# Sigmoid of the second expert choice formed as silu(x) / x in a fused mixture-of-experts kernel on Trainium2

## The reference, cut to what matters

```python
router_in = jnp.concatenate([x_flat, t_flat], axis=-1)
s = jax.nn.sigmoid((router_in @ W_router.T).astype(jnp.float32))
sel_scores = s + router_bias
_, topk_idx = jax.lax.top_k(sel_scores, TOP_K)
s_sel = jnp.take_along_axis(s, topk_idx, axis=1)
denom = jnp.sum(s_sel, axis=1, keepdims=True)
gates = jnp.where(denom > 1e-09, s_sel / (denom + 1e-09), 1.0 / TOP_K)
...
h = jax.nn.gelu(x_flat @ r_w1[e].T, approximate=False)
routed_out = routed_out + h @ r_w2[e].T * gates_full[:, e:e + 1]
```

## Time and profile before

| | us |
| --- | --- |
| median of 3 runs | 898.43 |
| lowest and highest | 897.16 and 898.77 |
| the profiled execution, its own time | 900.26 |
| its span from the first to the last instruction | 898.5 |
| TensorE busy in the span | 876.1 (98%) |
| VectorE busy | 683.7 (76%) |
| ScalarE busy | 576.5 (64%) |
| GpSimd busy | 408.5 (45%) |

### The profile page before, as it was taken

How to read it: one execution, slowest core, us unless ns; L and a number is a source line. 1 busy time by engine, 2 the same in 40 slices (tenths; PEclk the granted TensorE clock), 3 DMA queues, 4 the chain that set the end, 5 groups by cost and what they waited for, 6 DMA issues and landing times.

```text
span 898.5 us, 12685 instructions
## 1 busy us (share of the span) xinstructions
PE 876.1 (98%) x3878; PEld 694.5 (77%) x3878; DVE 683.7 (76%) x1097; ACT 576.5 (64%) x1032; POOL 408.5 (45%) x378
## 2 busy tenths in 40 slices
PE   8999999999999999999999999999999998999996
PEld 5678888878888888888888888888888785777773
DVE  7767777878689786686686686686766976998887
ACT  6878888765555455555555555555555677989896
POOL 7437785025256352253253253253222226755465
PEclk9999999999999999999999999999999999999999
DMA  9588982023023112012012012011010069182650
GB/s 311 174 259 274 321 278 97 1 85 132 19 77 109 36 47 82 1 47 82 1 48 82 1 48 82 5 42 48 7 42 1 0 105 178 36 182 54 158 107 35
DMA packets 35828, 82.96 MB, mean 92 GB/s; under 512 B 4400, under 2 KB 14256, under 8 KB 33840
## 3 DMA queue, kind: packets, MB, share of 16 engines
q1 hardware_dynamic: 35760, 82.15, 31.3%
HBM read 71.13 MB, written 6.83 MB: 87 GB/s over the span
## 4 chain that ended last, share of the span: by engine, by line
PE 77%; DVE 8%; ACT 4%; issue 4%; DMA 4%; SPq 2%; POOL 1%; DVEq 0%; ACTq 0%
PE ps L863 17%; PE ps L882 16%; PE ps L868 16%; PE ps L917 8%; PE ps L919 8%; PE ps L912 8%; DVE HL L1465 2%; DMA CWB<-scratch 2%; ACT HH L1005 1%; PE ps L899 1%; DVE HH L1462 1%; PE ps L897 1%; DVE Hf L1452 1%; POOL HL L1545 1%; SPq L722 1%
## 5 line engine op out<-in xcount | busy, mean ns | idle before, releaser
L999 ACT ACTIVATE Sg<-ps 128x512 f32<-128x512 f32 x288 | 171.7, 597 | 246.3 <-PE ps L882 245.9
L1445 DVE TENSOR_TENSOR Hf<-ps,Sg 128x512 f32<-128x512 f32 x288 | 198.1, 688 | 148.6 <-ACT Sg L999 94.0
L1545 POOL TENSOR_TENSOR HL<-Hf,HH 128x512 fp32r<-128x512 f32 x136 | 182.5, 1349 | 172.3 <-ACT HH L1005 154.6
L1005 ACT ACTIVATE HH<-Hf 128x512 fp32r<-128x512 f32 x346 | 216.4, 625 | 25.0 <-DVE Hf L1445 12.9
L1465 DVE TENSOR_TENSOR HL<-Hf,HH 128x512 fp32r<-128x512 f32 x242 | 215.3, 890 | 4.2 <-ACT HH L1005 3.2
L863 PE MATMUL ps<-XHL,WBH 128*128 128x512 f32 x512 | 203.7, 398 | 1.2 <-DVE Hf L1445 1.2
L882 PE MATMUL ps<-XHL,WBH 128*128 128x512 f32 x512 | 202.2, 395 | 0.0
L868 PE MATMUL ps<-XHL,WBL 128*128 128x512 f32 x512 | 202.0, 395 | 0.0
L1560 POOL TENSOR_TENSOR XT<-XT,TMP 128x512 f32<-128x512 f32 x64 | 84.2, 1316 | 251.4 <-DVE TMP L1341 251.4
L863 PEld LDWEIGHTS ps<-XHL,WBH 128*128 128x128 f32 x512 | 96.1, 188 | 25.2 <-DVE Hf L1445 2.3
L882 PEld LDWEIGHTS ps<-XHL,WBH 128*128 128x128 f32 x512 | 96.0, 188 | 23.1
(11 more groups left out here) (254 smaller groups left out, 1349.0 us busy)
## 6 DMA issues: line engine op xcount, KB each, us to landing
CWB<-scratch SPq DMA_DIRECT2D x68, 256.0 KB, 8.2
CWB<-scratch SPq DMA_DIRECT2D x15, 1024.0 KB, 4.7
GWD<-expert_down SPq DMA_DIRECT2D x21, 576.5 KB, 4.6
GWU<-expert_up SPq DMA_DIRECT2D x21, 514.0 KB, 4.9
ST<-in_wb_dram SPq DMA_DIRECT2D x8, 768.0 KB, 6.3
GX<-XT SPq DMA_DIRECT2D x68, 64.0 KB, 2.8
XT<-in_x_dram SPq DMA_DIRECT2D x8, 256.0 KB, 5.3
expert_up<-GWU SPq DMA_DIRECT2D x4, 512.0 KB, 4.4
```

The costliest lines, as they stand in the source:

```text
L999: e.activation(Sg[:, it.n % NG, :], zb[z % NZ][:, :], ACT.Silu).then_inc(s_act, 1)
L1005: e.activation(HH[:, it.n % NH, 0:it.cols], hidden_place(it), ACT.Copy).then_inc(s_hi_act, 1)
L1445: e.tensor_tensor(Hf[:, it.n % NS, :], zb[z % NZ][:, :], Sg[:, it.n % NG, :], ALU.mult).then_inc(s_prod, 1)
L1545: e.tensor_tensor(HL[:, it.n % NH, :], Hf[:, it.n % NS, :], HH[:, it.n % NH, :].bitcast(F32), ALU.subtract).then_inc(s_lo_pool, 1)
```

## The change

In both choices the sigmoid activation gives way to a silu activation. VectorE makes sigmoid(x) from it as silu(x) times 1/x. So that x is never near zero, it first adds 1e-14 to each score whose square is below 1e-30. These are five more instructions on VectorE for each choice: three in step 0 (square, test, add), ahead of the activation, which now waits for them, and two in step 1 (reciprocal, multiply).

```diff
                 if k in soft_b:
                     g = soft_b[k]
-                    e.wait_ge(*ab_done.of(("B", 4 * g + 3)))
-                    e.activation(pick_place(g)[0], LR[:, 16 * g:16 * g + 16, 0:8], ACT.Sigmoid).then_inc(s_exp, 1)
+                    e.wait_ge(s_ein, 4 + g)
+                    e.activation(pick_place(g)[0], LR[:, 16 * g:16 * g + 16, 0:8], ACT.Silu).then_inc(s_exp, 1)
...
                 desc = bc(S("desc8"), 1, s3)
+                x = LR[:, 16 * g:16 * g + 16, 0:8]
+                part = q0[:, 0:128].rearrange("p (t e) -> p t e", e=8)
+                if k == 0:
+
+                    e.wait_ge(*ab_done.of(("B", 4 * g + 3)))
+                    link(e.tensor_tensor(part, x, x, ALU.mult))
+                    after()
+                    link(e.tensor_scalar(part, part, 1e-30, 1e-14, ALU.is_lt, ALU.mult))
+                    after()
+                    e.tensor_tensor(x, x, part, ALU.add).then_inc(s_ein, 1)
                 if k == 1:
+                    e.wait_ge(s_ein, 4 + g)
+                    link(e.reciprocal(part, x))
                     e.wait_ge(s_exp, 4 + g)
                     e.wait_ge(f_scr[g][1 - g], 16)
+                    after()
+                    link(e.tensor_tensor(s, s, part, ALU.mult))
+                    after()
                     link(e.tensor_tensor(sel, s, bc(S("rb"), 1, s3), ALU.add))
```

## The result

| | before | changed |
| --- | --- | --- |
| median of 14 runs each, us | 898.07 | 901.42 |
| lowest and highest, us | 896.39 and 899.41 | 900.00 and 904.21 |
| ratio, 95% interval | | 1.0039 (1.0029 to 1.0049) |
| span of the profiled execution, us | 898.5 | 899.7 |
| mean granted clock of TensorE in it | 0.998 | 0.995 |

The changed kernel is 0.39% slower, 3.5 us, with an interval of 2.6 to 4.4 us (the two medians are 3.35 us apart). The forecast was 901.6, slower by 3.2 us. Mind the two spans, though: they differ by 1.2 us only.

A forecast was written before the change was run, and what follows sets the result against it. VectorE, with nothing to spare right behind each sigmoid, was taken to bound the kernel there. First place + 2.4 and second place + 0.8 us made + 3.2, from 898.43 to 901.6 us; range for 8 in 10: 899.0 to 903.0.

The forecast's parts named there:

- The first place: First choice (g = 0), last score to the store: + 2.4 us, bounds - 0.4 and + 3.0.
- the sum: Whole kernel: 2.4 us at the first choice plus 0.8 at the second, + 3.2 us, giving 901.6 us.
- Sg behind the end of the last score: First choice: Sg starts about 2.15 us after the last score, 1.66 before.
- Square: First choice, step 0: waits for GpSimd, ends 0.15 us after it, near 1.2 us instead of 0.29.
- Reciprocal: Step 1, 128 elements on VectorE: 0.98 us from the rows of 16 and 32 elements; lower bound 0.35.
- Multiplication: First choice, step 1: two SBUF inputs wait for GpSimd's L1545, so it takes 1.3 us.
- L1268's successor: First choice (L1283 in the changed kernel): no longer waits for GpSimd, 0.29 us instead of 0.77.
- Second place: Second choice (g = 1): Sg 0.50 us earlier, then 1.35 us more Vector work: + 0.8 us, bounds - 0.5 and + 1.1.
- the clock: Rival: TensorE's 2.8 us idle at the first choice lowers its clock, 2 to 3 us more, 904; chance 0.04.
- the stretch behind the store: Behind 718, store at 722.49 and gate DMAs: a later store pushes everything, nothing there can take a delay up.
- The loads win: Rival: extra Vector work hidden, Sg 0.4 us earlier at first choice, 0.5 or 1.0 at second: 897.0 to 897.5; chance 0.10.
- Bare instructions: Rival: VectorE pays its instructions without meeting GpSimd, + 1.0 us at first choice, + 0.4 at second: 899.8; chance 0.22.

The follow-up runs named there:

- e7: Changed kernel without square, test and add; 1e-30 added inside the score sum, reciprocal in step 0: 895.57 us against 897.57 for the kernel before, ratio 0.9978.
- e9: Changed kernel without square, test and add; 1e-30 added inside the score sum, reciprocal in step 1: 897.98 us against 897.25 for the kernel before, ratio 1.0004.
- e0: The changed kernel once more, unaltered, on another chip as a measure for follow-up runs: 901.13 us against 897.57 for the kernel before, ratio 1.0036.
- e6: Changed kernel with ten unread matmuls ahead of the product TensorE waits for at the first place: 900.01 us against 897.57 for the kernel before, ratio 1.0025.
- e2: The change made at the second place (g = 1) only: 898.08 us against 897.89 for the kernel before, ratio 1.0002.
- e3: Kernel before with Silu in place of Sigmoid in both choices, nothing added on VectorE: 894.73 us against 897.89, ratio 0.9964.
- after: The changed kernel's first measurement and profiled execution: median 901.42 us against 898.07 for the kernel before, ratio 1.0039.
- e8: Changed kernel with the HL behind the first choice written by VectorE instead of GpSimd: 900.23 us against 897.25 for the kernel before, ratio 1.0030.
- e1: The change made at the first place (g = 0) only: 900.85 us against 897.89 for the kernel before, ratio 1.0035.
- e5: Changed kernel without its two reciprocals: 897.82 us against 897.57 for the kernel before, ratio 0.9999.
- e4: Changed kernel with Sigmoid kept, so all added Vector instructions and all four loads are there: 903.98 us against 897.89 for the kernel before, ratio 1.0074.

## Why the prediction was right, point by point

**What bounds.** That VectorE is the engine with nothing to spare behind each activation held (e7 against e9: the reciprocal costs 2.1 us there), and so did the wait of ScalarE for step 0 (e9 against e0). The first place moved by + 2.22 us in e6, where the clock stayed up, and by + 2.37 in e0; the sum had 2.38. The second moved by + 0.76 to + 0.78; the sum had 0.85. In the time alone e2 leaves it between - 0.7 and + 1.2.

**Each term.** Sg behind the end of the last score: forecast 2.15 us, measured 695.42 - 693.38 = 2.04; the whole of the 0.11 us is that Sg starts before silu's row has ended. Square: until 0.15 us behind GpSimd, measured 0.15. Test: 0.20, measured 0.23. Reciprocal: 0.98 from the slope of two rows, measured 0.95. Multiplication: 1.3, measured 1.25. L1268's successor: 0.29, measured 0.28. TensorE's start behind the wait: 3.06 us after the one before, less the 0.23 of a normal step: 2.83, forecast 2.8. Second place: load to Sg 756.95 - 754.61 = 2.34 us against 2.88 in the earlier trace rows, - 0.54 (forecast - 0.50), and + 1.32 behind Sg (forecast + 1.35).

**Reciprocal and load.** The Trainium skill (VectorE: DVE Perf Modes, section the fixed hardware budget), eight repeats at 0.96 GHz, made an estimate of 1.15 us; the trace has 0.95, so the measurement decides against that estimate. The Trainium skill (ScalarE: Activation LUTs, What ACT_TABLE_LOAD costs) has a drain of about 1380 ns with each load. It isn't there either. In e3 the activation starts 0.01 us behind the end of the load, as in the earlier trace rows:

```profile
750.84 1.28 ACT L959 ACT_TABLE_LOAD   x1
752.13 0.28 ACT L959 ACTIVATE ps<-LR 128x128 f32<-128x128 f32 x1
```

**What was off, and what was luck.** The first is the clock. It stood in the forecast as a rival of 4 in 100 that would add 2 to 3 us, and at nothing in the sum. It fell in both profiled executions of the changed kernel and, by the mean clock, in about half of all or more, and on top of the forecast case, not in place of it. Its price was oversized: 1.0 us for the fall of 2.2 us, 2.8 for that of 6.8, both by the first gelu, and some 1 us in the median. Without the fall the change costs + 2.2 us by e6 (1.3 to 3.1), + 2.7 (after) and + 2.9 (e0) by the mean of those executions whose mean clock is 0.997 or more, short falls not excluded, and + 3.0 by the two stretches of e6's profile; e8, whose clock didn't fall either, has + 2.7 with 0.5 us less work. So the sum's + 3.2, which was meant for that case, is a few tenths to 1 us high, and the measured + 3.5 holds a term that the sum had at nothing. That the two agree to 0.3 us is in part luck.
The second is the stretch behind the store, of which the forecast said that nothing there can take a delay up. From the first copy to Sg it was 1.70 and 0.86 us shorter than before in the two profiles, of which 0.5 is the load at the second place. That looks like a delay taken up, but the other profiles speak for scatter of the DMAs. From the first copy to the start of the load at the second place it is 29.8 to 31.9 us in the thirteen kept profiles, and the longest of all is the one of the kernel before. The seven whose first place is over 1 us late have 31.0 us in the mean, the six others 30.9. Between the store of the gates and the first load of them lay 2.77 us before, 1.59, 3.20, 2.90 and 2.85 in after, e0, e1 and e2. So no profile shows that a late store is made up for, and the forecast's sentence stands as far as they reach; but a sum held against one profile must carry 1 us of scatter here.

**The rivals.** "The loads win" did not happen, but the loads are a larger prize than its - 0.9 to - 1.4 us: alone they bring 3.2 us (e3), which is more than the 1.27 and 0.4 us that the forecast let come back at most. That rival left step 0's three instructions ahead of the first silu, which eat all but 0.4 us there; without them Sg starts 0.44 us behind the last score instead of 1.85, and VectorE's full stretch with it, 1.40 us at this place. The prize was there, and e7 takes the part of it that the reciprocal and the multiplication leave. "Bare instructions" fell with the two meetings with GpSimd, both as forecast. e5 and e8 show what the forecast had argued: letting the multiplication slip past GpSimd only hands the wait to a later instruction, and only taking the work off GpSimd removes it.

## What to carry to other kernels

An added instruction costs its time in two cases: where its engine is full, and where another engine waits for its result. So look at busy time in the stretch of ten microseconds around it, and at who waits. The same reciprocal cost 1 us in a full stretch and nothing 2 us earlier, where VectorE waited for Sg and nobody waited for the reciprocal. The square, test and add stood in that same idle time and cost 2.7 us, since ScalarE waited for them. Look also at what GpSimd does at that moment: a wait that one moves off one instruction can fall on the next (e5). And a table load that the compiler has put ahead of a wait is paid for only in so far as it outlasts the wait.

## What the runs showed of the hardware

- VectorE instructions of 128 elements on each partition with two inputs in SBUF waited until GpSimd's running addition or subtraction had ended: 1.17, 1.25 and 1.35 us for 0.29 us of work, ended 0.15 us behind GpSimd; with GpSimd idle 0.29 (e8). The multiplication with an input in PSUM didn't (0.30 at 759.58, with GpSimd at work from 758.66 to 761.19), nor did the reciprocal of one SBUF input (0.95 us in e7 at 695.10, with GpSimd at work from 694.82, and 0.95 with GpSimd idle in e8).
- A fp32 reciprocal on VectorE: 0.25, 0.35 and 0.95 us for 16, 32 and 128 elements on each partition, 6.2 to 6.5 ns for each further element.
- Behind 2.7 us of idleness TensorE's granted clock fell from 2.4 to 1.2 GHz for 2 to 7 us in some executions and not in others (e4's profile). Kept busy with matmuls for nobody in that wait (e6), it didn't fall, nor did it behind waits of 1.68 us (e5) and 1.71 us (e8): 1.00 behind the wait in the three profiles, and a mean clock of 0.997 or more in all 31 runs.
- An ACT_TABLE_LOAD took 1.28 us, and where nothing else held the activation back it started 0.01 us behind the load (752.12 and 752.13 in e3).
- A scalar_tensor_tensor with one more addition took 0.19 us, as the tensor_tensor did.
